# A middle table of two tiles in the expert loop, and the last batch's routing spread further into it

## What is computed

```
h = layernorm(x) * (1 + ca) + sa;  x = x + ga * attention(h)      # 16 heads of 64, causal
h = layernorm(x) * (1 + cb) + sb
logits = h @ gate_w.T + expert_bias;  w, i = top_k(softmax(logits), 2);  w = w / (sum(w) + 1e-6)
for e in range(8):
    out += w_e * (gelu(h @ w_up[e].T) @ w_down[e].T)               # 128 -> 512 -> 128
x = x + gb * layernorm(out)
```

## Time and profile before

| | |
|---|---|
| median of 3 runs | 1037.58 us (1037.23 to 1043.69) |
| the profiled execution, its own time | 1033.38 us |
| its span in the trace | 1031.6 us |
| PE busy | 927.7 us (90%) |
| DVE busy | 840.1 us (81%) |
| ACT busy | 738.1 us (72%) |
| POOL busy | 590.3 us (57%) |
| mean granted clock of PE | 0.959 of full |

### The profile page before, as it was taken

How to read it: one execution, slowest core, us unless ns; L and a number is a source line. 1 busy time by engine, 2 the same in 40 slices (tenths; PEclk the granted TensorE clock), 3 DMA queues, 4 the chain that set the end, 5 groups by cost and what they waited for, 6 DMA issues and landing times. The chain is left out here.

```text
span 1031.6 us, 20590 instructions
## 1 busy us (share of the span) xinstructions
PE 927.7 (90%) x6138; PEld 663.8 (64%) x6138; DVE 840.1 (81%) x1740; ACT 738.1 (72%) x1993; POOL 590.3 (57%) x701
## 2 busy tenths in 40 slices
PE   5699999999999999999999999999998669999910
PEld 3467666666666667667666766676775558777700
DVE  7588888788888888888888888888887567998837
ACT  4487788778877887888787777877786635666614
POOL 1445556445765567576547765665763456665742
PEclk9799999999999999999999999999999889999965
DMA  7243334343334444334433334443333546665444
GB/s 242 81 112 103 98 90 110 96 116 95 90 105 113 106 115 113 101 90 108 120 105 107 105 109 106 112 120 102 90 97 86 207 149 229 232 228 201 169 128 123
DMA packets 123003, 129.18 MB, mean 125 GB/s; under 512 B 14019, under 2 KB 106072, under 8 KB 119824
## 3 DMA queue, kind: packets, MB, share of 16 engines
q1 hardware_dynamic: 116752, 116.10, 39.2%
q0 software_dynamic: 4992, 8.94, 2.6%
q10 hardware_dynamic: 1152, 2.85, 0.8%
HBM read 45.21 MB, written 40.41 MB: 83 GB/s over the span
## 5 line engine op out<-in xcount | busy, mean ns | idle before, releaser
L1335 POOL TENSOR_TENSOR four<-four 128x512 f32<-128x512 f32 x128 | 161.2, 1281 | 283.0 <-DVE ot L1277 152.4
L1142 ACT ACTIVATE prob<-ps,nmax 128x512 f32<-128x512 f32 (+3 forms) x512 | 264.4, 531 | 49.5 <-DVE nmax L1254 44.7
L1254 DVE TENSOR_REDUCE nmax<-ps 128x2 f32<-128x1024 f32 (+3 forms) x256 | 211.1, 825 | 8.8
L1061 PE MATMUL ps<-ident,prob 128*128 128x128 f32 x1280 | 192.3, 280 | 9.8 <-ACT probt L1163 5.1
L1061 PEld LDWEIGHTS ps<-ident,prob 128*128 128x128 f32 x1280 | 142.2, 141 | 60.7 <-ACT prob L1142 31.9
L1339 POOL TENSOR_TENSOR qk_lo<-four,qk_hi 128x512 fp32r<-128x512 f32 x128 | 162.5, 1292 | 1.9 <-ACT qk_hi L1170 1.9
L1247 DVE TENSOR_TENSOR ps<-ps,tri 128x256 f32<-128x256 f32 x256 | 109.5, 428 | 56.4 <-PE ps L1040 53.6
L1083 PE MATMUL ps<-probt,val 128*64 128x512 f32 (+3 forms) x1024 | 154.0, 443 | 0.5 <-ACT probt L1163 0.5
L1163 ACT COPY probt<-ps 128x512 f32<-128x512 f32 (+2 forms) x256 | 125.1, 523 | 22.9 <-PE ps L1061 20.1
L1170 ACT CAST qk_hi<-four 128x512 fp32r<-128x512 f32 x128 | 79.3, 622 | 82.6 <-POOL four L1335 82.6
L1870 POOL DMA_INDIRECT results<-y,to_i x92 | 102.9, 1118 | 49.8 <-issue 24.8
(11 more groups left out here) (256 smaller groups left out, 2204.7 us busy)
## 6 DMA issues: line engine op xcount, KB each, us to landing
four<-four SPq DMA_DIRECT2D x252, 128.0 KB
slots<-fill SPq DMA_DIRECT2D x64, 288.0 KB, 2.8
wt<-parts SPq DMA_DIRECT2D x15, 1024.0 KB
parts<-split SPq DMA_DIRECT2D x64, 128.0 KB, 2.3
wq_lo<-parts SPq DMA_DIRECT2D x8, 1024.0 KB
four<-slots SPq DMA_DIRECT2D x23, 288.0 KB
hb<-h_hi SPq DMA_DIRECT2D x64, 64.0 KB, 2.3
hb<-h_lo SPq DMA_DIRECT2D x64, 64.0 KB, 2.0
```

Source lines behind the costliest of these rows:

```text
L1061: mm = e.transpose(ps[:, PT + at % 2, at_block * P:(at_block + 1) * P], prob[:, unit, kk * P:(kk + 1) * P], ident[:])
L1142: e.activation(prob[:, unit, 0:w], ps[:, bank_s(idx) + j, 0:w], ACT.Exp, bias=nmax[:, q.par, idx, j:j + 1], accum_out=den[:, q.par, 2 * i ...
L1254: e.tensor_reduce(nmax[:, q.par, idx, :], ps[:, bank:bank + 2, 0:w], AX.X, ALU.max, negate=True).then_inc(v_max, 1)
L1335: e.tensor_tensor(qk[:, cols], tt[:, cols], ur[:, cols], op=ALU.add).then_inc(g_qk, 1)
```

## The change

Three tables instead of two. `MID_TILES` is 2: seven batches are sure to fill seven tiles, so tiles 5 and 6 get a table of their own after batch 6 (`tile_table(..., True)`, 21 DVE instructions in steps 1 and 2). It counts full tiles only, and adds its own tiles to `taken`. The last table then has 16 tiles instead of 18 and is made in steps 12 to 15 instead of 8 to 11.

The last batch's routing is spread:

| engine | step | before | after |
|---|---|---|---|
| PE | `r_logits`, `r_back`, `r_places` | 4, 5, 7 | 5, 6, 10 |
| ACT | `r_exp`, `r_rows` | 4, 5 | 6, 6 |
| DVE | `r_add` and `r_best`; `r_one` and `r_rest` | 4; 5 | 5; 7 |
| DVE | `r_second`, `r_two`, `r_cum`; `r_tails` | 6; 6 | 8; 9 |
| DVE | `r_at`; `r_slots` | 7; 7 | 10; 11 |

SP waits before tile 5 for the middle table and batch 6's scatters only, and before tile 7 for the last table and batch 7's. `r_keep` moves from before tile 4 to before tile 7. POOL scatters batch 7 after tile 0's results instead of before them.

```diff
+def full_tiles(batches):
+    return -(-(2 * batches * S - NX * (S - 1)) // S)
-EARLY_TILES = -(-(2 * EARLY * S - NX * (S - 1)) // S)
+EARLY_TILES = full_tiles(EARLY)
+MID_TILES = full_tiles(EARLY + 1) - EARLY_TILES
...
             def late_pe(e, g):
-                if g == 4:
+                if g == 5:
                     r_logits(e, LAST)
-                if g == 5:
+                if g == 6:
                     e.wait_ge(r_a, ROUTE_A * LAST + 1)
                     r_back(e, LAST)
-                if g == 7:
-                    e.wait_ge(r_row, LAST + 1)
+                if g == 10:
+                    e.wait_ge(v_y, 1)
                     r_places(e, LAST)
...
             def late_dve(e, g):
+                if g in (1, 2):
+                    tile_table(e, 2 * g - 2, True)
+                    tile_table(e, 2 * g - 1, True)
...
+            def before_turn(e, j):
+                if j == 0:
+                    e.wait_ge(r_row, LAST + 1)
+                if j == 1:
+                    e.wait_ge(r_base, B + 1)
...
                     for j in range(1, NTL):
-                        if j == EARLY_TILES - 1:
+                        if j == EARLY_TILES:
+                            e.wait_ge(r_t, MID_STEPS)
+                            e.wait_ge(d_x6, 16 * 2 * TB)
+                        if j == EARLY_TILES + MID_TILES:
                             r_keep(e, LAST)
-                        if j == EARLY_TILES:
                             e.wait_ge(v_table, 1)
-                            e.wait_ge(d_xl, 16 * 2 * TB * (B - EARLY))
+                            e.wait_ge(d_x7, 16 * 2 * TB)
                             e.wait_ge(d_none, 16)
...
-                            if q < IC:
-                                e.wait_ge(r_base, B + 1)
+                            before_turn(e, q // IC)
                             pe_y(e, q // IC)
...
                     r_scatter(e, LAST - 1, 0, 2 * TB)
-                    r_scatter(e, LAST, 0, 2 * TB)
                     for j in range(NTL):
+                        if j == 1:
+                            r_scatter(e, LAST, 0, 2 * TB)
```

More of the change, by code:

```diff
@@ L687, in first_loads @@
         def first_loads(e):
-            e.wait_ge(v_first, 1)
+            e.wait_ge(r_t0, 15)
             for p in range(2):
@@ L1513, in adaln_kernel, with tile_table @@
             y4 = sb(ph, "y4", [P, Y, TB, E])
-            def tile_table(e, part_):
-                done = r_t
+            MID_STEPS = 21
+            def tile_table(e, part_, mid):
+                n, at_, first_ = (MID_TILES, 0, 0) if mid else (REST, MID_TILES, MID_STEPS)
+                done, tick = r_t, Count(first_ + (0, 6, 11, 17)[part_])
                 full, heads, ends = (many[:, i, :] for i in range(3))
-                which, before, row, col = (tiles[:, i, :] for i in range(4))
+                which, before, row, col = (tiles[:, i, 0:n] for i in range(4))
+                begun_, after = begun[:, 0, 0:n, :], begun[:, 1, 0:n, :]
+                pick_, col_, row_ = pick[:, at_:at_ + n, :], table[:, 0, at_:at_ + n], table[:, 1, at_:at_ + n]
@@ L1528, in tile_table @@
-                    e.tensor_tensor(full, base[:], base0, op=ALU.subtract).then_inc(done, 1)
-                    e.wait_ge(done, 1)
+                    e.wait_ge(r_base, B if mid else B + 1)
+                    e.scalar_tensor_tensor(out=full, in0=base[:], scalar=-float(S) if mid else 0.0, in1=base0, op0=ALU.add,
+                                           op1=ALU.subtract).then_inc(done, 1)
+                    e.wait_ge(done, tick.after(1))
                     e.tensor_tensor(cross[:], full.unsqueeze(2).to_broadcast([P, NX, NX]),
-                                    steps.unsqueeze(1).to_broadcast([P, NX, NX]), op=ALU.is_gt).then_inc(done, 1)
@@ L1544, in tile_table @@
[L1544 to L1548, removed]
+                    e.tensor_tensor(begun_, by_expert(number[:, 0:n]), by_tile(ends), op=ALU.is_ge).then_inc(done, 1)
+                    e.wait_ge(done, tick.after(1))
@@ L1549, in tile_table @@
+                    e.tensor_tensor(after, begun_, by_tile(heads), op=ALU.mult).then_inc(done, 1)
+                    e.tensor_reduce(which, begun_, AX.X, ALU.add).then_inc(done, 1)
+                    e.wait_ge(done, tick.after(2))
+                    e.tensor_reduce(before, after, AX.X, ALU.add).then_inc(done, 1)
                     e.tensor_scalar(col, which, NX - 1.0, None, ALU.min).then_inc(done, 1)
                 if part_ == 2:
-                    e.wait_ge(done, 11)
-                    e.tensor_tensor(row, number[:, 0:REST], before, op=ALU.subtract).then_inc(done, 1)
@@ L1553, in tile_table @@
[L1553 to L1557, removed]
+                    e.tensor_tensor(row, number[:, 0:n], before, op=ALU.subtract).then_inc(done, 1)
+                    e.tensor_tensor(pick_, by_expert(col), by_tile(expert), op=ALU.is_equal).then_inc(done, 1)
@@ L1561, in tile_table @@
+                    e.tensor_reduce(before, begun_, AX.X, ALU.add).then_inc(done, 1)
                 if part_ == 3:
-                    e.wait_ge(done, 17)
                     e.tensor_tensor(row, row, before, op=ALU.add).then_inc(done, 1)
-                    e.wait_ge(done, 18)
+                    if mid:
+                        e.tensor_reduce(full, pick_.rearrange("p j x -> p x j"), AX.X, ALU.add).then_inc(done, 1)
+                        e.wait_ge(done, tick.after(2))
+                        e.tensor_tensor(taken, taken, full, op=ALU.add).then_inc(done, 1)
+                        e.scalar_tensor_tensor(out=row_, in0=row, scalar=float(S), in1=which, op0=ALU.mult,
+                                               op1=ALU.add).then_inc(done, 1)
+                        return
```

65 lines of the change are left out of this document (36 added, 29 removed).

## The result

The changed kernel takes 1042.52 us (median of 20 runs, 1036.85 to 1048.03), the kernel before 1036.3 us on the same chip (20 runs, 1034.01 to 1043.69). The ratio is 1.0058, with a 95% interval of 1.0042 to 1.0074: 6 us slower, where I had forecast 8.5 us less. The profiled execution took 1042.05 us with a span of 1040.2. On a second chip the ratio was 1.0051 (1.0022 to 1.008).

The account below looks back on a forecast made before the run. PE's stops and low clock from 810 to 860 us were taken as the bound: 16.0 us less 2.8, 2.3, 1.9 and 0.6, taken as 8.8, less 0.3 for tile 7, gives 8.5 and 1029.1 us; range 1023.5 to 1037.5.

Parts of the forecast that it names:

- ACT's stop: Before `pe_up` of tile 4, step 16: Gelus 3.92 and 5.23 us late with no cause named, expected to go with the scatter wait.
- the 5.70 us: PE's idle in step 16 before `pe_up` of tile 4, put down to the scatter wait and ACT's late Gelus, counted as removed.
- the 2.4 of low clock: PE from 850.96 to 856.95: matmuls and transposes at the lower clock after the step 16 stop, 2.4 us lost, counted as removed.
- rival A: Gelus 12 and 13: ACT's stop stays, bound to its place in the program; gain falls to 0.5 us, 1037; chance 0.24.
- The walk to step 12: Steps 1 to 12: middle table 3.55 us on DVE, `r_add` at 823.2, PE stops 2.8 us at `r_back`, 2.3 at `r_places`.
- The stops taken away: PE's stops in steps 7, 15 and 16 and the low clock: 4.69 + 1.14 + 5.70 + 2.1 + 2.4 = 16.0 us.
- Tile 5: SP's wait before tile 5's rows: no stop any more, SP comes to it at about 834.5, after batch 6's scatters landed.
- Tile 7: `pe_x(7)` waiting for batch 7's scatters: a stop of 0 to 2.2 us, 2.4 more if the clock falls; 0.3 taken.
- Rival B: Tile 7's wait becomes the bound: slow POOL issues and a 6.96 us landing cost 10.3 us, giving 1039; chance 0.06.
- POOL's backlog: Last five tiles: POOL's backlog gives back what the tiles' loop gains; against it, POOL catches up by about tile 8.
- rival D: No net gain: the tiles' loop gains but the last five tiles give it back, 1037; chance 0.03.
- The sum at the end: End of the loop: moves with PE, since the last results are bound to POOL's queue, which follows `dve_y` of tile 18.

Follow-up runs that it names:

- b_pool_old: The changed kernel with POOL's order as before, batch 7's eight scatters ahead of tile 0's results, on a chip with ACT's stops: 1048.31 us, ratio 1.0131.
- a_no_spread: The changed kernel with the last batch's routing at its old steps; middle table, tile 5's early start and POOL's new order stay: 1045.56 us, ratio 1.0086.
- run 20: Not a run's label but a count: with POOL's order as before in the changed kernel, POOL's unbroken run is 20 DMAs for 16; 1048.31 us.
- the runs with gaps: Both kernels with a small POOL operation behind each of 40 indirect DMAs: changed 1038.67 us (128x56) and 1032.29 (128x8), kernel before 1031.67 (128x56).
- the last group: 128x8 POOL operations to tile 19: kernel before 1030.13 us; changed kernel, middle table at step 6 and scatters ahead of tile 0's results, 1035.34.
- the fourth and fifth groups: Both kernels, and variants of the changed one, with small POOL operations behind 40 indirect DMAs, then to tile 19: ratios 1.0026 to 1.0089, then 0.993 and 0.9991.
- b_probe: The changed kernel with two one-column Gelus on ACT ahead of each Gelu of steps 10 to 19, on a chip with the stops: 1042.26 us, ratio 1.0039.
- a_tile5_waits: The changed kernel, but SP waits before tile 5 for the last table and all of batch 7's scatters, as before the change: 1034.06 us, ratio 1.0105.
- a_probe: The changed kernel with two one-column Gelus on ACT ahead of each Gelu of steps 10 to 19, on the chip without stops: 1025.02 us, ratio 1.0002.

## Why the prediction was wrong

- **The step that failed is that ACT's stop would go with the wait for the scatters**, which let the sum count the 5.70 us and the 2.4 of low clock behind it as taken away. Its return was rival A. I gave it 0.24 and a size of 7 us lost; it came with 17.0 us on ACT at Gelus 13 to 15, after 5.23 and a part of 3.92. I had bound it to a place in the program. It belongs to POOL's unbroken run, which the change made longer (16 DMAs for 12). My own walk had the run at 832.7 to 848.3 and asked only what it does to tile 7. The likely reason for the longer run: the spread routing gives the slots at 838 instead of 830, and the order on POOL puts tile 0's results ahead, so that tile 1's fall in at its end. Either seems to be enough: `b_pool_old` and `a_no_spread` each undo one of the two, still run 20 and 16, and keep the stops. Both undone together was not tried.
- **The walk to step 12 was right.** `r_add` started at 823.23 for 823.2; the middle table took 3.4 us (2.1 and 1.3) for 3.55, in two stretches of DVE, of which this is the first part's begin and the last one's end:

```profile
815.17 0.16 DVE L1544 SCALAR_TENSOR_TENSOR many<-base,const 128x8 f32<-128x8 f32 x1
...
820.29 0.15 DVE L1583 SCALAR_TENSOR_TENSOR table<-tiles 128x2 int32<-128x2 f32 x1
```

- **The stops taken away were mis-sized.** Of the 16.0 us, the 5.70 and most of the 2.4 behind it weren't gained: with POOL's run broken, that stop is 1.62, and with it whole the stops come back at another place. With the 5.7 and 2.4 out of it, and tile 5's 1.62 set off against tile 7's 1.63, the 8.5 become 0.4 us of gain; from tile 1 to tile 9 the runs with gaps show 0.2 with the 128x56 operation and 1.0 with 128x8 against it. That the two agree to a few tenths is luck, since single traces differ by more.
- **Tile 5** was right, without a stop. **Tile 7** (0 to 2.2, taken 0.3) was too small: 1.09 to 2.93 in the eight traces where ACT's stops don't hide it. Rival B had the right place, and the landing it needed, 6.96, was no exception: in those eight it is 5.0 to 8.4 us. The issues at 1.8 us each, which it needed too, didn't come.
- **POOL's backlog** (rival D, 0.03): it is the very run. I weighed only whether POOL catches up.
- **The sum at the end** moved as I had it, with PE: the results are read back at 1003.73 for 995.04.
- **The range** ended at 1037.5, 5 us below what was measured, and my only way to a loss beyond it was B. ACT's stop had a row with no releaser; I priced its return at its old size, and a stop of unknown cause has no such bound.

## What to carry to other kernels

A stop with no releaser in the trace is not a constant: before a change that moves work around it, look for what else runs each time it stands (here an unbroken run of POOL's DMAs that ended 1 to 3 us before the last stop did), and give its growth a chance of its own. When a wait is taken away, ask how much of the idle it really owned; two causes that end within 0.3 us of each other can't be told apart in one trace. Ask the same of the engine that a remedy burdens: the operations that ended the stops made POOL the bound of the last group. And compare marks inside the traces, not only totals: five totals in the fourth and fifth groups missed, while up to tile 9 the stops were gone as the theory had it.

## What the runs showed of the hardware

- On four of the six chips PE's counts reached ACT, DVE and SP late, up to 15.1 us (`b_probe`), while POOL issued 8 or more indirect DMAs 0.30 us apart. In the long runs ahead of 900 us the last stop ended 1.2 to 3.0 us after the last DMA. A 128x8 operation of POOL's between the DMAs, 0.21 us long, removed it. On a fifth chip the only such run inside the stretch, batch 6's eight scatters, had 1.62 us in one trace and nothing in the other. On the sixth, runs of 32 and more delayed nothing. What the counts and the DMAs share stays open, and so does why many runs of eight behind 860 and one of 20 at the end of the first trace (965.9 to 993.8, the largest space 0.39) show no stop or a small one.
- The same kernel takes 1024.9 to 1038.2 us from chip to chip (medians), more than the change is worth, so the kernels of one comparison have to share the chip.
- From the end of POOL's last scatter to SP's next issue it took 3.07 us in two traces and 3.06 in a third (`a_tile5_waits`), where SP's last weights of 1 MB had been issued 5.6 us or more ahead of that end. It took 5.0 to 8.4 in the eight traces of the changed kernel where they had been issued 1.2 to 3.7 us ahead of it (8.42 in `a_probe`), on chips with and without ACT's stops. That the weights are the cause fits these and wasn't tested.
